# Three-way attention pipeline on one core: the logit tile and the score tile of each TensorE step move ahead of the step's other matmuls

## The reference, cut to what matters

```python
xn = _ln(x, norm_s_w, norm_s_b)
spatial_out = _spatial_experts(xn, idx_s, ...)      # called S: softmax(q k^T) v, then out_w
xt = _ln(x, norm_t_w, norm_t_b)
temporal_out = _temporal_experts(xt, idx_t, ...)    # called T: the same, causal, xt added
fused = _cross_mha(spatial_out, temporal_out, ...)  # called C: q from S, k and v from T
x = x + fused
```

## Time and profile before

| | |
|---|---|
| median of 3 runs | 1627.6 us (1627.55 to 1627.78) |
| the profiled execution: own time, span | 1629.0 us, 1627.2 us |
| PE, DVE, ACT, POOL busy, share of the span | 93%, 76%, 69%, 61% |
| granted TensorE clock, mean of the span; from 400 to 1300 us | 0.947; 1.00 |
| first S, T, C score tile of one round, and of the next S slot | 816.13, 840.55, 864.93, 889.50 us |

### The profile page before, as it was taken

One profiled execution on the slowest core, in us unless ns is written; L12 is line 12 of the kernel. 1 busy time (PEld: TensorE's weight loads), 2 busy tenths in 40 slices (PEclk: granted clock), 3 DMA queues, 4 the chain that ended last, 5 costly groups with the idle time before them and its releaser, 6 DMA issues. The chain is left out here.

```text
span 1627.2 us, 37445 instructions
## 1 busy us (share of the span) xinstructions
PE 1510.4 (93%) x8694; PEld 661.2 (41%) x8694; DVE 1241.3 (76%) x3412; ACT 1129.1 (69%) x2201; POOL 1000.1 (61%) x1359
## 2 busy tenths in 40 slices
PE   4779948899999999999999999999999999975999
PEld 1239932233333333343333333333333343211777
DVE  6868858579888887979888887979788888452772
ACT  5756734567787878787787878787787878824433
POOL 7704443856777776866767776856767775432553
PEclk9879958889999999999999999999999999967999
DMA  3311153645654655655655655655655643030222
GB/s 83 105 31 46 46 81 50 87 71 74 80 81 61 88 69 65 86 69 72 80 77 64 88 65 69 85 68 74 80 75 66 88 59 64 2 40 28 59 71 65
DMA packets 140021, 110.34 MB, mean 68 GB/s; under 512 B 22721, under 2 KB 134465, under 8 KB 139969
## 3 DMA queue, kind: packets, MB, share of 16 engines
q1 hardware_dynamic: 137920, 105.53, 44.0%
q0 software_dynamic: 2048, 4.20, 1.0%
HBM read 19.29 MB, written 8.39 MB: 17 GB/s over the span
## 5 line engine op out<-in xcount | busy, mean ns | idle before, releaser
L1170 ACT ACTIVATE probs<-psum 128x512 f32<-128x512 f32 (+3 forms) x1536 | 755.2, 548 | 226.8 <-PE psum L1285 216.2
L1070 DVE TENSOR_REDUCE mx_S<-psum 128x1 f32<-128x512 f32 x512 | 326.2, 681 | 47.5 <-PE psum L1265 45.8
L1070 DVE TENSOR_REDUCE mx_C<-psum 128x1 f32<-128x512 f32 x512 | 317.8, 676 | 45.1 <-PE psum L1265 45.1
L1066 DVE CUSTOM_DVE_ANT_0 psum<-psum,causal 128x128 f32<-128x128 f32 (+3 forms) x512 | 242.8, 510 | 100.6 <-PE psum L1265 97.8
L1265 PE MATMUL psum<-ks_S,qs_S 96*128 96x512 bf16 x512 | 196.9, 395 | 10.3 <-DMA ks_S<-parts_k 6.0
L1265 PE MATMUL psum<-ks_C,qs_C 96*128 96x512 bf16 x512 | 199.6, 398 | 4.3 <-DMA ks_C<-parts_k 1.2
L1285 PE MATMUL psum<-qs_C,ks_C 99*128 99x512 bf16 x512 | 189.3, 385 | 3.6 <-ACT probs L1170 3.2
L1285 PE MATMUL psum<-qs_S,ks_S 99*128 99x512 bf16 x512 | 190.6, 384 | 0.2
L951 POOL CAST parts_q<-f_q 128x512 bf16<-128x512 f32 x48 | 29.3, 610 | 227.6 <-ACT f_q L1161 227.1
L1265 PE MATMUL psum<-ks_T,qs_T 96*128 96x128 bf16 (+3 forms) x512 | 156.7, 309 | 1.7 <-DVE mx_S L1070 0.9
L1285 PE MATMUL psum<-qs_T,ks_T 99*128 99x256 bf16 (+3 forms) x512 | 153.3, 305 | 2.1 <-ACT probs L1170 1.0
(11 more groups left out here) (186 smaller groups left out, 2723.3 us busy)
## 6 DMA issues: line engine op xcount, KB each, us to landing
qs_S<-parts_q SPq DMA_DIRECT2D x96, 128.0 KB, 4.4
ks_S<-parts_k SPq DMA_DIRECT2D x96, 128.0 KB, 5.1
qs_T<-parts_q SPq DMA_DIRECT2D x96, 128.0 KB, 4.4
ks_T<-parts_k SPq DMA_DIRECT2D x96, 128.0 KB, 4.6
qs_C<-parts_q SPq DMA_DIRECT2D x96, 128.0 KB, 4.5
ks_C<-parts_k SPq DMA_DIRECT2D x96, 128.0 KB, 4.9
w_in_S<-in_s_in SPq DMA_DIRECT2D x16, 257.0 KB, 2.7
w_in_T<-in_t_in SPq DMA_DIRECT2D x16, 257.0 KB, 2.7
```

Source lines behind the costliest of these rows:

```text
L1066: nc.vector.tensor_tensor_reduce(tile[:, 0:last_key], tile[:, 0:last_key], causal[:, T - last_key:T], 1.0, NEG, ALU.add, ALU.max, mx[kind] ...
L1070: nc.vector.tensor_reduce(mx[kind][:, n:n + 1], tile, AX_X, ALU.max, negate=True).then_inc(reduced, 1)
L1170: nc.scalar.activation(probs[:, group_place(kind, b, n // 4), n % 4, t0:T], psum[:, LOGITS + ring_place(kind, b, n, RC), t0:T], ACT.Exp, s ...
```

## The change

Within each step, `logits` and `score` are issued first; then come T-turn, projection, value sums and output, in their old order. Nothing is added or removed, and no other engine's list changes.

```diff
                     for n in range(TILES):
+                        if n < LAG and exists(bo):
+                            logits(ko, bo, TILES - LAG + n)
+                        if n >= LAG and exists(bb):
+                            logits(kb, bb, n - LAG)
+                        if exists(ba):
+                            score(ka, ba, n)
                         if n == TURN_AT[0]:
                             turn_maxima(ka, ba, 0)
                         if n == TURN_AT[1]:
...
                         for c in range(3):
                             if 0 <= n - PROJECT_AT[c] < PROJECT_PARTS[c]:
                                 project(kn, bn, c, n - PROJECT_AT[c])
-                        if n < LAG and exists(bo):
-                            logits(ko, bo, TILES - LAG + n)
-                        if n >= LAG and exists(bb):
-                            logits(kb, bb, n - LAG)
                         q, rest = divmod(n - LAG - WEIGH_AFTER, 4)
                         if rest == 0 and q < 0 and exists(bo):
                             weigh(ko, bo, q + 8)
                         if rest == 0 and q >= 0 and exists(bb):
                             weigh(kb, bb, q)
-                        if exists(ba):
-                            score(ka, ba, n)
                         if 0 <= n - OUTPUT_AT < OUTPUT_PARTS and exists(bo) and ko != "S":
                             output(ko, bo, n - OUTPUT_AT)
```

## The result

The changed kernel takes 1645.0 us (median of 4 runs, 1642.65 to 1646.25) against 1627.6 us before: ratio 1.0102, 95% interval 1.0089 to 1.0115. It is slower by 17.4 us, outside the range on record. The profiled execution is the fastest of the four (1642.65 us, span 1640.9).

A forecast was written before the change was run, and what follows sets the result against it. TensorE was taken to bound the S and T slots, DVE the C slot from its middle on. Terms -0.15 - 0.17 + 0.14 + 0.04 + 0.18 = +0.04 us per round, x 14 = +0.6, gave 1628.2 us; range 1622.5 to 1634.0.

The forecast's parts named there:

- T and S slots, loss: Step 9: score 9 waits for reduction 6, holding back projection and sums; +0.14 us in T slot, +0.04 in S slot.
- Output behind sums: Step 29, S and T slots: first output part takes 0.53 us instead of 0.44, together +0.18 us per round.
- The T slot's gain: Score 21 ahead of sums, so `swap` and reciprocal come earlier and logit tile 29 isn't late: -0.17 us per round.
- The C slot's gain: Score 14 goes earlier, VectorE starts reduction 14 at 877.98 instead of 878.19: -0.15 us per round.
- Rival 3: Slower: bank-waiting scores hold back projection and sums, C slot steps 21, 25, 29; +0.6 us per round, 1636 us; chance 0.20.
- Nothing at: Value sums (W) directly behind the projection (P): the same 0.09 us gap as behind a logit tile.

The follow-up runs named there:

- e5: The changed kernel with `swap` cut to 128 of its 512 columns, work left out: 1633.0 us, ratio to the kernel before 1.0026.
- e6: The kernel before (old order) with `swap` cut to 128 of its 512 columns, work left out: 1619.1 us, ratio 0.9940.
- e9: The changed kernel with projection and sums ahead of the score at steps 9 and 25 alone: 1625.9 us, ratio to the kernel before 0.9991.
- e4: The changed kernel with the sums ahead of the score at step 29 alone: 1639.3 us, ratio to the kernel before 1.0067.
- e8: The kernel before with one score, that of step 21, ahead of the sums: 1624.9 us, ratio 0.9977.
- e3: The changed kernel with the T-turn back at the head of its step: 1633.5 us, ratio to the kernel before 1.0034.

## Why the prediction was wrong, step by step

The sum had +0.04 us per round; measured were +1.28, in the S slot +0.54, in the T slot +0.74, in the C slot 0.00.

- **The step that failed is the term "T and S slots, loss".** It had +0.18 us per round, all of it at step 9. The runs show about +1.2: 0.71 at step 9, 0.43 at step 25 and 0.10 at step 29.
- **At step 9 it was mis-sized.** The mechanism was named, with +0.14 us in the T slot and +0.04 in the S slot, and that `keep_maxima` stays put was nearly so (0.11 and 0.01 us later). I had the T-turn land 0.28 us after its start; `keep_maxima` begins 0.43 us after it (849.91 to 850.34), as a reduction does after its score. Reduction 6 ended 6.61 us into the T slot, where I had 6.44, score 9 followed it by another 0.06, for which I had nothing, and the wait was 0.36. The projection behind it adds 0.19 where 0.05 was lost already. Together about +0.50 in the T slot. In the S slot the wait is 0.33 against 0.12 lost there before: +0.21. My bounds, 0.30 and 0.15, were both too narrow, and the S slot's +0.04 was not worked out at all. The old trace had the rows for it: score 8 goes at 821.70, so that score 9 would want to go at 822.14, and reduction 6, the first of three behind `keep_maxima`, is done at 821.75 + 0.60 = 822.35:

```profile
821.55 0.27 DVE L1080 TENSOR_SCALAR ng<-psum 16x128 f32<-16x128 f32 x1
821.75 1.86 DVE L1070 TENSOR_REDUCE mx_S<-psum 128x1 f32<-128x512 f32 x3
```

- **Step 25 was not in the sum.** "I follow what that does at the places where an engine waits" looked at the waits of the old trace. Step 25 had no wait there, because W ran while `swap` and the reduction behind it held VectorE. The lead of one tile put score 25 ahead of W and opened it: +0.20 us in the S slot, +0.23 in the T slot. e5 against e6 shows it for the S slot, e9 that steps 9 and 25 together hold the whole loss.
- **Output behind sums** was right in size: +0.10 in each of two slots, +0.18 on record. e4 gave it back, with a wait of 0.10 at score 29 of the T slot, which was not in the sum either.
- **The T slot's gain** of 0.17 was right (e8: 0.19).
- **The C slot's gain** of 0.15 didn't show. As said, VectorE's last idle time lies ahead of reduction 14, but that one starts 0.06 us earlier than before and not 0.21: VectorE idled 0.91 us for its T-turn, and score 9, for which I had no wait, waited 0.16. With the T-turn first the gain was 0.22 (e3).
- **The T slot and the S slot added up:** 0.50 + 0.23 + 0.10 (output) + 0.10 (score 29) - 0.17 = 0.76 against 0.74; and 0.21 + 0.20 + 0.10 + 0.09 (score 1, which now waits for the C slot's last reductions) - 0.04 (score 28 waits no more) = 0.56 against 0.54.
- **Rival 3** was the outcome, by its mechanism, but I put its place mainly in VectorE's half of the C slot. There the same waits are longest (0.78 us at score 25) and cost nothing: VectorE's stock did not run out, it never idles from reduction 14 on, and the slot is as long as before. The cost lies in the slots which TensorE bounds.
- **Nothing at** W behind P: 0.09, as said. The Trainium skill ("TensorEngine Tiling (Array Packing)", Key Properties) says that changing the tiling mode drains the TensorE. Both orders have the same number of such changes, so by that rule alone an output part behind sums costs nothing more; the trace has 0.10 us, and the measurement decides.

## What to carry to other kernels

On an in-order engine that sets the pace, put the instruction that may have to wait for another engine behind long work that is ready to go, not ahead of it. When a stream is moved by one place, waits open where the old trace shows none, because they were covered: list for every long block which not yet free buffer its neighbours need, in every slot, and not only where the old profile has an idle time. A long wait on the engine that isn't the bound is no sign of cost, a short one on the bound is.

## What the runs showed of the hardware that was not expected

An fp32 projection behind a bf16 score of 256 columns that itself had to wait took 1.05 us to the next sums and began 0.20 us after the score, instead of 0.95 and 0.11: 0.19 us on top of the wait. Behind a score of 512 columns that had to wait it took 0.95 (S and C slots). An fp32 output part took 0.54 us behind value sums and 0.44 behind a bf16 score. The transpose of 16 columns reached VectorE 0.43 us after its start. Two traces of the same kernel differ by 1.5 us in where the first part of `attend` ends, with a granted clock of 0.59 and 0.74 in the same 20 us; whether one is the cause of the other is open.
